# Gated attention on one Trainium2 core: the selected tokens' rows fetched by an indirect DMA in place of products with one-hot tables

## The reference

```python
q, k, v = split(x @ w_qkv.T)            # 16 heads of 64
gate scores = MLP(layernorm(mean of q over heads))          # one per token
topk_vals, topk_idx = top_k(scores, 32)
scores = full(-1e9).at[topk_idx].set(topk_vals);  gate = sigmoid(scores)
dots = q k^T / 8 * gate_i * gate_j;  out = softmax(dots) v @ w_out.T + b_out
```

## Time and profile before

| | |
|---|---|
| median of 3 runs | 682.26 us (681.39 to 684.41) |
| the profiled execution | 683.05 us |
| its span | 681.3 us |
| busy: PE, DVE, ACT, POOL | 548.2, 507.4, 360.6, 267.5 us |
| gated stage, TensorE's first instruction to its last | 139.3 to 215.9 us |

### The profile page before, as it was taken

How to read it: one execution, slowest core, us unless ns; L and a number is a source line. 1 busy time by engine, 2 the same in 40 slices (tenths; PEclk the granted TensorE clock), 3 DMA queues, 4 the chain that set the end, 5 groups by cost and what they waited for, 6 DMA issues and landing times. The chain is left out here.

```text
span 681.3 us, 11830 instructions
## 1 busy us (share of the span) xinstructions
PE 548.2 (80%) x3800; PEld 308.0 (45%) x3800; DVE 507.4 (74%) x2314; ACT 360.6 (53%) x738; POOL 267.5 (39%) x499
## 2 busy tenths in 40 slices
PE   1866468928968799867999999999999898899870
PEld 1865367817757566311233333333333355465320
DVE  6599999371273687788989999999999055379784
ACT  5841134500120376611478878888887755466762
POOL 2001007720002266810244545545454454266774
PEclk9996675555987699855599999999999899899996
DMA  8000000000000038420011111111120000000001
GB/s 316 1 1 1 0 1 1 0 1 0 1 1 1 0 122 227 155 78 3 4 35 32 47 49 36 32 36 36 32 63 3 7 1 1 2 0 16 32 16 62
DMA packets 17580, 24.77 MB, mean 36 GB/s; under 512 B 3246, under 2 KB 14014, under 8 KB 17342
## 3 DMA queue, kind: packets, MB, share of 16 engines
q1 hardware_dynamic: 16942, 21.91, 10.6%
q10 hardware_dynamic: 576, 2.10, 0.9%
HBM read 13.65 MB, written 10.35 MB: 35 GB/s over the span
## 5 line engine op out<-in xcount | busy, mean ns | idle before, releaser
L905 DVE CUSTOM_DVE_ANT_0 w_qkvT<-d_pS,w_qkvT 128x512 bf16<-128x512 f32 x480 | 203.9, 486 | 16.9 <-PE d_pS L896 12.0
L1577 ACT ACTIVATE d_P<-pT 128x768 f32<-128x768 f32 (+1 forms) x192 | 165.9, 882 | 63.2 <-PE pT L1603 61.6
L1457 POOL TENSOR_SCALAR_AFFINE_SELECT d_P<-d_P 128x256 f32<-128x256 f32 x256 | 102.7, 415 | 134.2 <-ACT d_P L1577 134.1
L896 PE MATMUL d_pS<-Ks,Qs 48*128 48x512 bf16 x480 | 98.1, 325 | 12.8 <-DVE hadamard L905 8.9
L1603 PE MATMUL d_pO<-d_P,V 128*32 128x512 f32 (+3 forms) x1024 | 99.9, 466 | 1.4 <-POOL d_P L1457 0.9
L1603 PE MATMUL pT<-Qs,Ks 51*128 51x512 bf16 (+3 forms) x512 | 72.7, 312 | 2.0 <-ACT d_mT L1547 2.0
L896 PEld LDWEIGHTS d_pS<-Ks,Qs 48*128 48x128 bf16 x480 | 32.2, 96 | 56.1 <-DVE hadamard L905 51.9
L1603 PEld LDWEIGHTS pT<-Qs,Ks 51*128 51x128 bf16 x512 | 20.8, 95 | 75.0 <-ACT d_P L1577 43.7
L905 DVE DVE_READ_ACCUMULATOR2_ANT hadamard<- 128x1 f32 x512 | 42.5, 83 | 0.0
L1603 PEld LDWEIGHTS d_pO<-d_P,V 128*32 128x32 f32 x1024 | 21.3, 111 | 32.7 <-issue 29.8
L453 POOL MEMSET a_expS<- 1x1024 f32 x4 | 3.8, 945 | 78.6 <-DVE a_q L263 78.6
(11 more groups left out here) (317 smaller groups left out, 1082.1 us busy)
## 6 DMA issues: line engine op xcount, KB each, us to landing
Qs<-q_stack SPq DMA_DIRECT2D x32, 192.0 KB, 3.0
q_stack<-Qp SPq DMA_DIRECT2D x8, 384.0 KB, 2.6
X<-in_x_dram ACTq DMA_DIRECT2D x4, 512.0 KB, 6.2
q_stack<-Qp SPq DMA_DIRECT2D x8, 256.0 KB, 2.5
out_dram<-e_moe SPq DMA_DIRECT2D x8, 256.0 KB, 2.0
w_qkvT<-in_w_qkvT_dram SPq DMA_DIRECT2D x1, 1536.0 KB
Ks<-k_stack SPq DMA_DIRECT2D x32, 48.0 KB, 3.2
q_stack<-Qp SPq DMA_DIRECT2D x8, 128.0 KB, 2.1
```

The costliest lines, as they stand in the source:

```text
L896: last = nc.tensor.matmul(dst[:, at:at + w], top.Qs[c][rows, h % 8, 128 * q:128 * q + 128], top.Ks[c][rows, h // 4 % 2, 0:w], start=True, ...
L905: last = nc.vector.tensor_tensor_reduce(out=junk[:, at:at + w], in0=src[:, at:at + w], in1=top.wide_mask[:, 512 - w:512], scale=1.0, scala ...
L1457: last = nc.gpsimd.affine_select(out=view, in_=view, compare_op=ALU.is_ge, fill=0.0, base=0, pattern=[[0, 2], [1, 128]], channel_multiplie ...
L1577: nc.scalar.activation(P[pair % 4][:, :, P_AT[unit]:P_AT[unit] + w], pT[(3 * pair + unit) % 2][:, :, 0:w], ACT.Exp, scale=float(HD4) ** -0 ...
```

## The change

The first stage stores each chunk of N3 to a table in DRAM, `n3_rows`, one row of 512 bytes for each token. In the gated stage MAX_INDEX gives the positions of the eight largest in each round. They are converted to fp32, spread over a table by batch (`wide_index`) and turned into one number per partition by a product with ones, for two groups Q of 4 batches x 32 tokens; the batch offset is added as they are written as whole numbers (`row_at`). GpSimd fetches the 128 rows of each group by an indirect DMA into G[Q]. The gate is now computed from the 32 best scores alone and takes the same way to one number per partition. One product for each group with a table of 260 columns (128 with the gate on the diagonal, 128 plain, 4 that sum a batch's tokens with the factor -1/480) gives what the one-hot tables gave. The sum over all tokens is a product of its own, one column for each tile. `selT` is compared with the token number directly. Three of the five weight preparations move into the gated stage, the other two and the loads of their tables are gone. The query/key products wait for `gq` in the first half and for `gv` only in the second. TensorE gets 4 busy products behind the sums and 10 behind the gate products.

```diff
+                for c in chunks:
+                    sp.wait_ge(sm["s3_n"], done[c])
+                    sp.dma_start(dram["rows_store"](c), n[c].rearrange("p (b r) d -> p b (r d)", r=R))\
+                        .then_inc(top.rows_stored, 16)
...
-                other_weights()
...
+            def _(sp):
+                sp.dma_start(tables[:, :], dram["tables"]).then_inc(sm["tables"], 16)
+                for Q in range(NQ):
+                    sp.dma_start(weights[Q][:, D:2 * D + 4], dram["ident_less"]).then_inc(sm["tables2"], 16)
...
+                pool.wait_ge(top.rows_stored, 16 * CHUNKS)
+                pool.wait_ge(sm["rows"], 1)
+                for Q in range(NQ):
+                    nc.gpsimd.indirect_dma_start(G[Q][:, :], None, dram["rows"],
+                                                 bass.IndirectOffsetOnAxis(ap=row_at[:, Q:Q + 1], axis=0))\
+                        .then_inc(rows_in[Q], 16)
...
+                    nc.vector.max_index(index8[:, best], top8[:, best], src[:, :]).then_inc(sm["index8"], 1)
+                    if t < TOP_K // 8 - 1:
+                        nc.vector.match_replace(SC[(t + 1) % 3][:, :], top8[:, best], src[:, :], LOWEST)\
+                            .then_inc(sm["replaced"], 1)
...
+                dve.wait_ge(sm["place_psum"], 1)
+                nc.vector.tensor_tensor(row_at[:, :], P0[:, 2, 0:NQ], tables[:, S:S + NQ], ALU.add).then_inc(sm["rows"], 1)
...
-                for b in range(B):
-                    pe.wait_ge(sm["sel"], b + 1)
-                    for r in range(R):
-                        last = mm(P0[:, b // 4, 128 * (b % 4):128 * (b % 4) + NSEL], top.N3[:, R * b + r, :],
-                                  SEL[:, R * b + r, :], r == 0, r == R - 1)
-                last.then_inc(sm["gather_psum"], 1)
...
+                for b in range(B):
+                    for r in range(R):
+                        last = mm(P1[:, 1, b:b + 1], top.N3[:, R * b + r, :], one[:, 0:1], r == 0, r == R - 1)
+                last.then_inc(sm["total_psum"], 1)
+                keep_busy(P0[:, 3, :], 4)
+                pe.wait_ge(sm["wide_index"], 1)
+                for Q in range(NQ):
+                    last = mm(P0[:, 2, Q:Q + 1], wide_index[:, 4 * Q:4 * Q + 4, :], one[0:B, 0:1])
+                last.then_inc(sm["place_psum"], 1)
+                pe.wait_ge(sm["wide_gate"], 1)
+                for Q in range(NQ):
+                    last = mm(P0[:, 2, NQ + Q:NQ + Q + 1], wide_gate[:, 4 * Q:4 * Q + 4, :], one[0:B, 0:1])
+                last.then_inc(sm["gate_psum"], 1)
+                keep_busy(P0[:, 3, :], 10)
+                pe.wait_ge(sm["weights"], NQ)
+                pe.wait_ge(sm["tables2"], 16 * NQ)
+                for Q in range(NQ):
+                    pe.wait_ge(rows_in[Q], 16)
+                    last = mm(P0[:, Q, 0:2 * D + 4], G[Q][:, :], weights[Q][:, :])
+                last.then_inc(sm["gather_psum"], 1)
+
+                pe.wait_ge(sm["gq"], 1)
                 for half in range(2):
+                    if half:
+                        pe.wait_ge(sm["gathered"], 1)
```

More of the change, by code:

```diff
@@ L20 @@
 TOP_K = 32
-NSEL = 2 * TOP_K + 2
 LOWEST = -3e38
@@ L584, in gated_attention_phase @@
         sm = ph.sems(
-            "scores_psum scores_row top8 replaced mask_row zeroed tok_psum tok mask_bf exp_gate gate_den gate rank_psum rank_sub "
-            "rank rank_rows_psum rank_rows rank_wide selT plain sel gather_psum nonsel bars gathered "
+            "scores_psum scores_row top8 index8 replaced zeroed one tables tables2 index_f wide_index place_psum rows place_out "
+            "exp_gate gate_den gate wide_gate gate_psum gate_col weights selT total_psum others gather_psum gq bars gathered "
             "qk_psum qk_out qk_out_a v_psum v_out c_psum c_out yuc_psum yu_copy yu dy "
@@ L591, in gated_attention_phase @@
         SC = [ph.sb(f"SC{j}", [B, S]) for j in range(3)]
[L592 to L601, removed]
+        top8 = ph.sb("top8", [B, TOP_K])
+        index8 = ph.sb("index8", [B, TOP_K], mybir.dt.uint32)
+        index_f = ph.sb("index_f", [B, TOP_K])
+        egate = ph.sb("egate", [B, TOP_K])
+        gden = ph.sb("gden", [B, TOP_K])
+        gate = ph.sb("gate", [B, TOP_K])
+        wide_index = ph.sb("wide_index", [B, B, TOP_K])
+        wide_gate = ph.sb("wide_gate", [B, B, TOP_K])
+        one = ph.sb("one", [128, 2])
+        tables = ph.sb("tables", [128, S + NQ])
+        row_at = ph.sb("row_at", [128, NQ], mybir.dt.uint32)
+        token = ph.sb("token", [128, NQ])
+        gate_col = ph.sb("gate_col", [128, NQ])
+        rows_in = [ph.sem(f"rows_in{Q}") for Q in range(NQ)]
+        G = [ph.sb(f"G{Q}", [128, D]) for Q in range(NQ)]
+        weights = [ph.sb(f"weights{Q}", [128, 2 * D + 4]) for Q in range(NQ)]
+        others = ph.sb("others", [128, B])
         gq = ph.sb("gq", [128, B, TOP_K])
@@ L694, in _ @@
-                nc.vector.tensor_copy(gq[:, :, :], G[:, :, 0:TOP_K])
-                dve.wait_ge(sm["bars"], 1)
-                nc.vector.tensor_tensor(gv[:, :, :], G[:, :, TOP_K:2 * TOP_K], bcast(means[:, 1, :], TOP_K),
-                                        ALU.subtract).then_inc(sm["gathered"], 1)
+                nc.vector.reciprocal(gate[:, :], gden[:, :]).then_inc(sm["gate"], 1)
+                dve.wait_ge(sm["gate"], 1)
+                nc.vector.tensor_tensor(wide_gate[:, :, :], by_batch(gate[:, :]), own, ALU.mult).then_inc(sm["wide_gate"], 1)
@@ L698, in _ @@
+                last.then_inc(sm["gathered"], 1)
+                nc.vector.tensor_scalar(top.gate_expT[:, :], top.gate_expT[:, :], top.norm_w[:, 1:2], None, ALU.mult)
                 dve.wait_ge(sm["qk_psum"], 1)
@@ L802, in _ @@
-                for r in range(1, R):
-                    for r2 in range(r):
-                        last = mm(P1[:, 0, r * B:r * B + B], top.ones_bf[:, :], mask_bf[:, r2, :], False,
-                                  r == R - 1 and r2 == r - 1)
-                last.then_inc(sm["rank_psum"], 1)
-                pe.wait_ge(sm["rank"], 1)
-                for r in range(R):
-                    last = nc.tensor.transpose(P1[0:B, 1, 128 * r:128 * r + 128], rank[:, r, :], top.ident[:, :])
-                last.then_inc(sm["rank_rows_psum"], 1)
@@ L2102 @@
     m_rows = nc.dram_tensor("m_rows", (2, 3, 2, HEADS // 2, S), BF16, kind="Internal").ap()
+    n3_rows = nc.dram_tensor("n3_rows", (B * S, D), FP32, kind="Internal").ap()
+    dram["rows"] = n3_rows
+    dram["rows_store"] = lambda c: n3_rows[CT * 128 * c:CT * 128 * c + CT * 128].rearrange("(b p r) d -> p b (r d)", p=128, r=R)
     def stack_load(stack):
```

120 lines of the change are left out of this document (45 added, 75 removed).

## The result

The changed kernel takes 674.03 us (median of 4 runs, 672.94 to 675.80), the kernel before 682.75 (median of 4, 681.39 to 684.41): ratio 0.9869, 95% interval 0.9847 to 0.9892. The forecast was 674.8 (671 to 680). The profiled execution has a span of 672.2 us where before had 681.3.

What follows compares the result with a forecast made beforehand. The gated-attention stage's path through VectorE, TensorE, then VectorE again was taken as the bound. Preparations 1.4, earlier query/key start 4.7 and clock 1.4 summed to 7.5 us saved, giving 674.8 us, range 671 to 680.

Steps and rivals of the forecast that it cites:

- Step 1, preparations: End of the first stage: five VectorE weight preparations leave it, a gain of 1.4 us.
- Step 2, selection: VectorE's selection with MAX_INDEX at 0.76 us each: ready 10.6 us after the first score transpose, 13.7 at the upper bound.
- Step 3, TensorE's queue: Sums (13.9 us) and 4 busy products delay index products to 16.3 us after the first score transpose; row_at written at 17.15.
- Step 4: Beside the fetch: gate chain, gate products and 10 busy products leave TensorE free 22.15 us after the first score transpose.
- Step 5, the fetch: GpSimd's two indirect DMAs land 5.5 us after row_at, bounds 2.1 to 12.4, just behind the busy products.
- Step 6, gather: Four-instruction gather takes 1.7 us; query/key products start 24.8 us after the first score transpose instead of 29.5, gaining 4.7.
- Step 7, the clock: Query/key products: one microsecond at half clock instead of 4.6, a gain of 1.4 us, bounds 0 and 1.9.
- the late clock: Rival: TensorE's clock rises as late as before in the query/key products; gain 6.1 us, 676.2 us; chance 14%.
- The fetch behind VectorE's passes: Rival: GpSimd's fetch waits for VectorE's short passes, gather 1.7 us later; gain 5.8 us, 676.5 us; chance 12%.
- the late fetch: Rival: fetch lands 7 to 13 us from row_at, clock gain gone; at 9 us, 679.7 us; chance 12%.
- the slower case: Rival: fetch takes over 15 us, TensorE waits for rows_in; at 16 us, 686.7 us; chance 5%.
- The sums at full clock: Rival: TensorE's sums take 7.4 us and VectorE becomes the bound; 5.7 us more gain, 669.1 us; chance 7%.

Runs made afterwards that it cites:

- e2: Changed kernel with its three remaining weight preparations put back at the end of the first stage; 674.96 us, ratio 0.9888.
- e3: Changed kernel with 22 sum calls ahead of the index products and 10 behind the gate products, replacing both groups of busy products; 672.51 us, ratio 0.9846.
- e9: Changed kernel plus four unused VectorE SBUF-to-SBUF copies of 128x2048 right behind row_at and token; 680.32 us, one execution.
- e1: Changed kernel without the 10 busy products behind the gate products; 675.13 us, ratio 0.9879.
- e5: Changed kernel with both groups fetched once into spare tiles ahead of the real fetches, four indirect DMAs instead of two; 676.79 us, ratio 0.9912.
- e8: Changed kernel plus two unused VectorE SBUF-to-SBUF copies of 128x2048 right behind row_at and token; 674.87 us, one execution.
- e7: Changed kernel plus five unused VectorE copies of 8x512 from PSUM to SBUF right behind row_at and token; 674.40 us, one execution.
- e6: Changed kernel plus eight unused VectorE SBUF-to-SBUF copies of 128x512 right behind row_at and token; 679.02 us, one execution.
- b1: Changed kernel with GpSimd pre-adding four batches, 20 sum calls, gate chain earlier, no four busy products, twelve behind gate products in their own bank; 665.81 us, ratio 0.9747.

## Why the prediction was right, point by point

- *Step 1, preparations*: 1.4 forecast, 1.32 measured; the three of them in e2 are worth 1.01. The wait for the stores to DRAM never showed.
- *Step 2, selection*: MAX_INDEX 0.75 each with its load (0.76 forecast), ready at t = 10.34 (10.6). Hidden, as said: VectorE waited 6.58 us (5.7 forecast, 5 to 6 as a sign): 5.46 for TensorE's queue and 1.12 for the index products themselves, which the forecast left out of the wait.
- *Step 3, TensorE's queue*: the sums took 13.58 (13.7 to 13.9), the index products started at t = 15.80 (16.3). From their start to row_at's start were 1.12 us, where I took 0.65 after the mask transposes, so row_at stands at t = 16.92 to 17.08 (17.15): two small errors that cancel. e3 showed that this queue, not VectorE, decides.
- *Step 4*: TensorE free at t = 22.38 (22.15).
- *Step 5, the fetch*: 4.91 us from the end of row_at to landing (5.07 from its start), forecast 5.5 with bounds of 2.1 to 12.4. The total came near partly by luck: no row had the price of an issue, and the forecast took 1.6 for two issues, 3.2 to land and 0.7 on a guess for addressing 256 rows. Measured were 0.90 from the end of row_at to the first issue, 1.5 from one issue to the next, and 2.5 to land. Not adding the port's rule to the sum was right for these passes, and only for these: e9 shows the hold.
- *Step 6, gather*: 1.30 to the copy of gq, forecast 1.7, since the clock rose inside it. Query/key products from t = 24.16 (24.8): gain 5.31, not 4.7.
- *Step 7, the clock*: the mis-sized term. I took one microsecond of query/key products at half clock and 1.4 us of gain; they had none, and gained 2.27, above even my upper bound of 1.9, which multiplied ten instructions by too small a difference (9.28 - 7.01 us from start to start is what all 32 at full clock give). So they took 7.17 us, below the 7.5 to 8.5 that I gave as a sign.

Together 1.32 + 5.31 + 2.27 = 8.90 of the 9.1 us in the span, where the sum said 7.5; by the medians of this comparison it is 8.7. The forecast of the time, 674.8, lies nearer to the 674.03 than the gain does, since the kernel before came out 0.5 us slower here (682.75) than where I counted from (682.26). Of the rivals, the late clock is what e1 turns into: in its execution the clock rose later without the busy products. The fetch behind VectorE's passes, the late fetch and the slower case didn't come, as the fetch landed 0.4 us before TensorE came to it. The sums at full clock didn't come either: they took 13.65 us, 213 ns each, here and in e1, and the clock was 0.50 in every window from 138 to 152. The rule of the Trainium skill, TensorE: Matmul & The Clock Gate, "Part 1", that sustained activity releases the throttle, does not hold for these rows, as it didn't for the gather of before.

## What to carry to other kernels

Ask of a replaced product not only how long it is but what it must wait for: 64 instructions of 213 ns cost what the 64 before did, and yet the change gains, since the sums need nothing of the selection and the gather proper became four instructions. Ask also what stands between a product and its reader: 2.8 us lay there before that lie elsewhere or nowhere now. Before an indirect fetch from DRAM, find 5 us of work that needs doing anyway or keeps TensorE's clock up; without it the wait can be paid a second time in the products behind it, as in e5. Long SBUF-to-SBUF passes of VectorE don't belong beside the issue of such a fetch.

## What the runs showed of the hardware that I had not expected

- An indirect fetch of 128 rows of 512 bytes keeps GpSimd busy for 1.21 us (the first) and 0.94 to 0.96 (the next), and lands 2.4 to 2.8 us after its issue in the runs without copies from SBUF beside it, also with two more in flight (e5). With the four long copies (e9) the two land 3.1 and 3.4 us after their issues.
- VectorE's 128x2048 copy from SBUF to SBUF (1.18 us) holds the fetch instruction until the copy ends, three times to 0.12 or 0.13 us after it (e8, e9); copies of 8x512 from PSUM don't (e7).
- The clock can fall again in a pause of a few microseconds: in e5 TensorE was busy for 0.42 to 0.66 us in each window of one microsecond from 160 to 164, with the clock at 0.85 to 1.00, and in those from 164 to 167 it was 0.50.
- The meanv products take 5.14 to 5.33 us in e1, e6 and b1 and 3.66 with the change, because the clock fell to 0.50 in them (windows 176 to 179, 179 to 182 and 170 to 172; with the change it stayed at 1.00). Why it fell there, behind the same 0.89 us of idle time, stays open.
